# Last network of a graph kernel: each set's sum is added at its segment by TensorE, and the last group of edges has four sets in place of five

## What is computed

```python
x1 = x_nodes[src].reshape(-1, N_SEG, EXTENT)          # 16 segments of 32
x2 = x_edges.reshape(-1, N_SEG, EXTENT)
i1, i2, i3 = (path_indices[:, 0], path_indices[:, 1], path_indices[:, 2])
contrib = path_coeffs[None, :, None] * x1[:, i1, :] * x2[:, i2, :]
edge_out = jnp.zeros((x2.shape[0], N_SEG, EXTENT), x_nodes.dtype).at[:, i3, :].add(contrib)
out = jnp.zeros((n_nodes, OP_SIZE), x_nodes.dtype).at[dst].add(edge_out.reshape(-1, OP_SIZE))
```

## Time and profile before

| | us |
|---|---|
| median of three runs | 857.91 |
| profiled execution, its own time | 857.5 |
| its span, first to last instruction | 855.7 |
| busy: TensorE products / weight loads | 775.5 / 501.2 |
| busy: VectorE / ScalarE / GpSimd | 611.4 / 217.7 / 129.7 |
| mean granted TensorE clock | 0.968 of 2.4 GHz |

### The profile page before, as it was taken

How to read it: one execution, slowest core, us unless ns; L and a number is a source line. 1 busy time by engine, 2 the same in 40 slices (tenths; PEclk the granted TensorE clock), 3 DMA queues, 4 the chain that set the end, 5 groups by cost and what they waited for, 6 DMA issues and landing times.

```text
span 855.7 us, 10601 instructions
## 1 busy us (share of the span) xinstructions
PE 775.5 (91%) x2972; PEld 501.2 (59%) x2972; DVE 611.4 (71%) x1581; ACT 217.7 (25%) x456; POOL 129.7 (15%) x145
## 2 busy tenths in 40 slices
PE   6888898898898999999999999889889997997998
PEld 2556455365365766667567554565676673683673
DVE  8876675675676534553553553799999999999895
ACT  6633123123121311311312212203304304304300
POOL 6000000000101000000000002611531451340000
PEclk9899999999999999999999999899989997997999
DMA  5813323214131423433342100742523443330000
GB/s 198 306 58 103 111 84 124 108 53 159 61 124 69 142 87 130 149 115 117 117 147 75 62 1 31 256 132 77 183 86 99 126 120 98 108 89 1 0 1 25
DMA packets 39175, 88.38 MB, mean 103 GB/s; under 512 B 3890, under 2 KB 4159, under 8 KB 39135
## 3 DMA queue, kind: packets, MB, share of 16 engines
q1 hardware_dynamic: 34496, 72.71, 25.2%
q0 software_dynamic: 4640, 15.21, 6.0%
HBM read 86.86 MB, written 1.05 MB: 103 GB/s over the span
## 4 chain that ended last, share of the span: by engine, by line
PE 51%; DVE 24%; issue 15%; DVEq 7%; ACT 1%; POOL 1%; DMA 0%; ACTq 0%; SPq 0%; POOLq 0%
PE PS L753 40%; DVE big L1504 8%; PE PS L1043 6%; DVE tail L1495 4%; DVEq L1470 3%; DVE tail L1514 2%; DVE prods L1514 2%; DVEq L1474 2%; DVE h L1128 1%; PE PS L909 1%; PE PS L762 1%; DVEq L1504 1%; DVEq L1514 1%; PE PS L858 1%; PE PS L954 1%
## 5 line engine op out<-in xcount | busy, mean ns | idle before, releaser
L753 PE MATMUL PS<-big 128*128 128x512 f32 (+1 forms) x368 | 137.2, 524 | 1.7 <-DVE big L1398 1.7
L1495 DVE SCALAR_TENSOR_TENSOR tail<-big,coef 128x448 f32 (+3 forms) x216 | 130.7, 616 | 3.1 <-issue 3.1
L1504 DVE TENSOR_TENSOR big<-big,tail 128x448 f32 (+3 forms) x216 | 120.9, 560 | 4.1 <-DVE tail L1495 3.1
L753 PEld LDWEIGHTS PS<-big 128*128 128x128 f32 x368 | 67.4, 190 | 63.6 <-issue 54.8
L753 PE MATMUL PS<-hT,big 128*128 128x256 f32 (+1 forms) x512 | 87.0, 329 | 4.4 <-ACT hT L678 4.4
L576 POOL DMA_INDIRECT big<-h_rows,src_i x58 | 77.2, 1331 | 85.6 <-PE PS L1043 62.9
L753 PEld LDWEIGHTS PS<-hT,big 128*128 128x128 f32 x512 | 77.5, 191 | 15.2 <-ACT hT L678 7.3
L550 POOL TENSOR_TENSOR rstd<-var,minus_half 128x1 f32<-128x1 f32 x36 | 21.6, 601 | 421.3 <-DVE var L1102 419.2
L1043 PE MATMUL PS<-big,hotd_more 128*128 128x512 f32 x176 | 76.5, 592 | 0.0
L1057 PE MATMUL PS<-hotd_more,tail 128*128 128x256 f32 x256 | 59.5, 387 | 0.0
L1043 PEld LDWEIGHTS PS<-big,hotd_more 128*128 128x128 f32 x176 | 33.4, 190 | 41.6 <-issue 41.6
(11 more groups left out here) (206 smaller groups left out, 1043.6 us busy)
## 6 DMA issues: line engine op xcount, KB each, us to landing
big<-in_edge_attr_dram SPq DMA_DIRECT2D x32, 512.0 KB, 3.6
big<-in_L_gnn_vn_W_dram SPq DMA_DIRECT2D x12, 1024.0 KB, 5.3
big<-in_L_gnn_m_w_dram SPq DMA_DIRECT2D x8, 1024.0 KB, 5.4
big<-in_L_gnn_gcn_W_dram SPq DMA_DIRECT2D x7, 1024.0 KB, 5.2
big<-in_L_gnn_wv_dram SPq DMA_DIRECT2D x4, 1024.0 KB, 5.3
big<-in_L_gnn_wq_dram SPq DMA_DIRECT2D x4, 1024.0 KB, 5.3
big<-in_L_gnn_wk_dram SPq DMA_DIRECT2D x4, 1024.0 KB, 5.6
big<-in_L_gnn_wo_dram SPq DMA_DIRECT2D x4, 1024.0 KB, 5.3
```

Of the source, the lines that this page charges most:

```text
L753: return pe.matmul(o, lhsT, rhs, start=start, stop=stop)
L1495: dve.scalar_tensor_tensor(out=prod[:, slot, tiles, :], in0=xs[:, tiles, bass.ds(i1, EXT)], scalar=coef[:, row:row + 1], in1=xe[:, tiles, ...
L1504: dve.tensor_tensor(o, o, prod[:, slot, tiles, :], ALU.add)._wait_ge(path_step, max(product_at[slot], added_at[0])).then_inc(path_step, 1)
```

## The change

It does three things. TensorE no longer turns a set's sum; for each set, each half t of the nodes and each of its four segments q it multiplies set_sums (stationary, 128x128) by 32 columns of the identity (moving), and the result is added in PSUM bank t at the segment whose address it reads from a register. These are the banks into which the tile products go. VectorE's 32 additions and the semaphore sums_turned go. In the last group four blocks have a set (4 to 7) in place of five, so 48 rows are summed there, and VectorE's order of blocks is 4, 0, 5, 1, 6, 2, 7, 3. TensorE loads the 32 addresses ahead of the groups.

```diff
-         [3, 0, 4, 1, 5, 6, 7, 2]]
-SETS_OF = [8, 6, 5, 5, 5]
+         [4, 0, 5, 1, 6, 2, 7, 3]]
+SETS_OF = [8, 6, 5, 5, 4]
...
-            def turn_sums(lo, hi):
+            places = [pe.alloc_register(f"place{i}") for i in range(4 * SETS)]
+            pe.wait_ge(setcoef_set, 1)
+            pe.load(places, set_path[:])
+
+            def place_sums(lo, hi):
 
                 for n in range(lo, hi):
                     pe.wait_ge(sums_out, hi)
                     k = OUT_ORDER[n]
                     for t in range(NT):
-                        ins = pe.transpose(set_bank(k)[:, t * P:(t + 1) * P], set_sums[:, k, t * P:(t + 1) * P], ident[:])
-                    ins.then_inc(sums_turned, 1)
+                        for q in range(4):
+                            at = pe.snap(places[4 * k + q], min_val=0, max_val=(SEGS - 1) * EXT)
+                            pe.matmul(PS[:, t, bass.ds(at, EXT)], set_sums[:, k, t * P:(t + 1) * P],
+                                      ident[:, q * EXT:(q + 1) * EXT], start=False, stop=True, skip_group_check=True)
...
                     if g == GROUPS - 1 and i:
-                        turn_sums((0, 2, 4, 5)[i - 1], (2, 4, 5, 6)[i - 1])
-            turn_sums(6, 7)
+                        place_sums((0, 2, 4)[i - 1], (2, 4, 6)[i - 1])
+            place_sums(6, 7)
             sum_tiles(GROUPS - 1, 0, SPLIT_TILE, STEP_AT[GROUPS - 1] + 2 * SUMMED_OF[-1])
-            turn_sums(7, 8)
+            place_sums(7, 8)
             sum_tiles(GROUPS - 1, SPLIT_TILE, SIZES[-1], STEP_AT[GROUPS])
...
-            set_regs = [r for some in regs for r in some][0:4 * SETS]
-            dve.load(set_regs, set_path[:])
-            for at, k in enumerate(OUT_ORDER):
-                dve.wait_ge(sums_turned, max(at + 1, (2, 2, 4, 4)[at] if at < 4 else 0))
-                turned = set_bank(k).rearrange("p (t c) -> p t c", t=NT)
-                for q in range(4):
-                    o = x[:, :, bass.ds(bounded(set_regs[4 * k + q]), EXT)]
-                    link(dve.tensor_tensor(o, o, turned[:, :, q * EXT:(q + 1) * EXT], ALU.add))
             for t in range(NT):
                 dve.wait_ge(tile_summed, ET)
                 dve.tensor_tensor(x[:, t, :], PS[:, t, :], x[:, t, :], ALU.add).then_inc(final, 1)
```

More of the change, by code:

```diff
@@ L327, in gnn_stack_kernel @@
             sem, ["h_ready", "hot_squared", "hotd_ready", "acc_zero", "path_step", "tile_summed", "final"])
-        set_ready, set_used, setcoef_set, sums_out, sums_turned = map(
-            sem, ["set_ready", "set_used", "setcoef_set", "sums_out", "sums_turned"])
+        set_ready, set_used, setcoef_set, sums_out = map(
+            sem, ["set_ready", "set_used", "setcoef_set", "sums_out"])
         h_rows = nc.dram_tensor("h_rows", (N, D), F32, kind="Internal").ap()
```

## The result

The changed kernel takes 870.03 us (median of four runs, 865.79 to 872.98) against 858.26 us before (four runs); the ratio is 1.013 with a 95% interval of 1.0094 to 1.0166. The forecast was 864.7 us in a range of 860.5 to 871.5, slower. The profiled execution took 868.1 us; its span is 866.3 us, 10.6 more than before. Over the four runs the time goes with the granted clock of the whole execution: 865.79 and 868.10 us at 0.968, 871.96 at 0.961 and 872.98 at 0.959. Where the two longer ones lost clock isn't recorded; what follows is read from the execution of 868.1 us.

What follows compares the result with a forecast made beforehand. TensorE was taken as the bound of the last group, with VectorE within a microsecond. Placing +14.3, turns -1.7, a set -5.2 and the wait -0.6 gave +6.8 us on 857.9, so 864.7 us, range 860.5 to 871.5.

Steps and rivals of the forecast that it cites:

- VectorE's 32 additions were covered: Last group: the 32 additions of turned sums, 11.47 us, lie under 20.7 us of TensorE tiles; removal gains nothing.
- The placing, 14.3 us: Last group on TensorE: 128 records for eight sets at 0.112 us each add 14.3 us.
- The lower end: Placing record on TensorE: a quarter of 0.112 us for a quarter of the moving columns, 0.028 us; rival's chance 0.17.
- Registers at no cost: Placing products on TensorE: an address from a register adds no time, read from one earlier product.
- The upper end of 0.36 us: Placing products on TensorE: 0.36 us each, as VectorE's register-addressed additions take; the end +15.5 us, 873.4 us.
- VectorE 2.5 us later: Last group: four more rows of sums start VectorE's last set at 823.1 in place of 820.54, 2.5 us later.
- P: TensorE's time to place one set's sums, 16 records, forecast 1.79 us; below 1.48 VectorE would be the bound.
- its other check: Last set of the last group: TensorE wants it at 825.3, VectorE has it ready at 825.1, so no wait.
- A set, the turns and the wait, -7.5 us: Last group on TensorE: one set fewer -5.2 us, turns gone -1.7, the wait before the tiles gone 0.6.
- The clock: TensorE in the placing: array streaming a quarter of the time loses granted clock, one fall +3.0 us, 867.7; chance 0.08.
- its own signs of being wrong: Wrong if TensorE waits at tiles' first half, placing records stand apart, or clock below 1.0 from 812 to 858 us.
- dearer records: Placing: load and stream don't overlap, 0.14 us a record, +10.3 us, or the sequencer sets the pace, +15.5; chance 0.24.

Runs made afterwards that it cites:

- the spread kernel: Changed kernel with the same 64 placing products, one or two ahead of each tile's product of sets 5 to 7 and each last-group tile; 863.94 us, ratio 1.0097.

## Why the prediction was right or wrong

*VectorE's 32 additions were covered: right.* They are gone and nothing moved forward; VectorE is idle 23.09 us at the end. No run takes them away alone, but the 11.6 us add up without a term for them.

*The placing, 14.3 us: right, 14.0.* The choice of the nearest row, 0.112 us a record with 128 moving columns, gave 0.109 with 32. The reason given, that the load of 128 stationary columns sets the pace, was an argument and is now shown by the kernels that vary one operand each, at fixed addresses (0.1116 us with 128 moving columns, 0.109 with 32, 0.034 with 32 stationary ones). The lower end, 0.028, and the rule of the Trainium skill (TensorE: Matmul & The Clock Gate, section "Back-to-back issue gap", 25 ns for up to 64 moving columns) are far from it: the rule's gap has no load, and here each record has one.

*Registers at no cost: right.* Fixed addresses give the same 60.83 us. The upper end of 0.36 us was no danger. TensorE's load of the 32 registers lies in its wait before the first set of group 1, which is 3.34 us before and 3.35 after.

*VectorE 2.5 us later: right in size.* 14.88 us between third and last set, forecast 14.98. TensorE never waited for it in the changed kernel. The 2.9 us of the kernel with four sets and no placing, forecast 2.6, agree. But the place of the wait was wrong. The prediction looks for it at the first half of the tiles and lets VectorE decide from P below 1.48 (its own terms, 823.3 + 7P against 833.2, give 1.41). By its other check, 812.96 + 4P + 5.18 against 825.1, TensorE waits for the last set already below 1.74, and there both kernels waited that did, 5.83 and 4.24 us. With the measured P, 16 x 0.109 = 1.74, the changed kernel was on that edge.

*A set, the turns and the wait, -7.5 us: right.* With them the sum at full clock is 6.5 us, forecast 6.8, and the spread kernel, which holds the clock, takes 55.83 us from the first set on: 6.6 above before.

*The clock: the step that failed.* It was a rival with a chance of 0.08 and a price of 3.0 us, set aside with "TensorE isn't idle in the new order". TensorE was not idle, and the clock fell all the same, twice, for 5.1 us together: almost half of the loss. (A clock below 1.0 between 812 and 858 us was among its own signs of being wrong.) The rows showed one fall behind a wait, and I took the wait for the cause; that a busy engine with little moving through it can lose its clock was in no row of the kernel before. So the predicted +6.8 us is what the spread kernel does (6.6 in the stretch), and the changed kernel lost 11.8 by the medians and is near the range's upper end. That 870.03 us still lies within the range is partly luck: the range was drawn that wide for dearer records, which did not come, and for one fall of 3.0 us, where there were two for 5.1.

## What to carry to other kernels

Price a small product by the operand that sets its pace: with a fresh float32 load of 128 columns a record costs 0.11 us whether 32 or 128 columns move, so four products for four segments cost eight records where a transpose costs one. Do such products in small portions between full ones, or make them move more columns: in bursts of 32 and 48 records they cost the clock of the work behind them here, all but the first burst. And before moving work from one engine to another, look which of the two ends last there; additions that end half a microsecond under a cover of 20 us of TensorE work are worth nothing.

## What was not expected of the hardware

The granted clock fell to half while TensorE was busy without a gap: behind the second burst of 32 records with 32 moving columns (0.57 in 824.20 to 827.40) and in the burst of 48 (0.55 in 834.60 to 837.80, 0.50 up to 841.50). With 128 moving columns at the same pace, with transposes of 128 columns, and with the same thin records spread, it stayed at 1.00. The first burst of 32 had no fall behind it in the three kernels that have such bursts (the changed one, fixed addresses, five sets), the second had one in all three, and so had the third of the kernel with five sets, each in one profiled execution. Why the first has none stays open, as does how much thin work in a row would be borne.
